# Two of eight products of an LSTM's second half, moved behind the first half's last group on TensorE

## The reference, cut to what matters

```
xW = jnp.einsum('ntd,dg->ntg', x, Wx) + b
def step(carry, xw_t):
    prev_h, prev_c = carry
    A = xw_t + prev_h @ Wh                    # Wh is 512 x 2048: gates i, f, o, g
    i, f, o = sigmoid(A[:, 0:H]), sigmoid(A[:, H:2*H]), sigmoid(A[:, 2*H:3*H])
    g = jnp.tanh(A[:, 3*H:4*H])
    next_c = f * prev_c + i * g
    next_h = o * jnp.tanh(next_c)
    return ((next_h, next_c), next_h)
```

## Time and profile before

| | |
|---|---|
| median of 3 runs | 3955.26 us |
| lowest, highest | 3949.76, 3957.27 us |
| the profiled execution | 3956.3 us |
| its span in the trace | 3954.5 us |
| TensorE's granted clock, mean | 0.994 of full speed |

### The profile page before, as it was taken

How to read it: one execution, slowest core, us unless ns; L and a number is a source line. 1 busy time by engine, 2 the same in 40 slices (tenths; PEclk the granted TensorE clock), 3 DMA queues, 4 the chain that set the end, 5 groups by cost and what they waited for, 6 DMA issues and landing times.

```text
span 3954.5 us, 255717 instructions
## 1 busy us (share of the span) xinstructions
PE 3651.2 (92%) x110802; PEld 3082.3 (78%) x110802; DVE 3272.8 (83%) x19153; ACT 1751.2 (44%) x8244; POOL 774.6 (20%) x3624
## 2 busy tenths in 40 slices
PE   6899999999999999999999999999999999999875
PEld 4688788888888888888888888888888888877764
DVE  5588888888888888888888888888888888888766
ACT  3244444444444444444444444444444444444432
POOL 0122122222222222222222222222222222212111
PEclk8999999999999999999999999999999999999999
DMA  7100000000000000000000000000000000000000
GB/s 272 48 7 7 10 10 10 7 7 10 10 10 10 7 9 7 10 10 10 10 7 7 10 10 10 10 7 9 7 10 10 10 10 7 7 7 7 6 6 8
DMA packets 19109, 63.32 MB, mean 16 GB/s; under 512 B 3958, under 2 KB 4526, under 8 KB 14914
## 3 DMA queue, kind: packets, MB, share of 16 engines
q1 hardware_dynamic: 17692, 46.67, 3.7%
q10 hardware_dynamic: 294, 0.33, 0.0%
HBM read 38.48 MB, written 8.39 MB: 12 GB/s over the span
## 4 chain that ended last, share of the span: by engine, by line
DVE 51%; PE 44%; issue 4%; ACT 1%; DMA 1%; SPq 0%; ACTq 0%; DVEq 0%; POOL 0%; POOLq 0%
PE ps_lstm L1013 34%; DVE lstm_sums L738 18%; DVE lstm_arg L743 7%; DVE lstm_ig_fc L749 6%; DVE rnn_sums L847 5%; DVE lstm_gates_2c L754 5%; DVE lstm_h_parts L778 3%; PE ps_rnn L1052 3%; DVE lstm_h_scaled L771 2%; DVE lstm_h_parts L774 2%; PE ps_lstm_in_b L1094 2%; PE ps_ssm L1094 2%; PE ps_lstm_in_b L1155 1%; PE ps_lstm_in_a L1155 1%; PE ps_x L1149 1%
## 5 line engine op out<-in xcount | busy, mean ns | idle before, releaser
L1013 PE MATMUL ps_lstm<-lstm_Wh_parts,lstm_h_parts 128*20 128x256 f16 x65472 | 1972.1, 273 | 252.2 <-DVE lstm_h_parts L778 247.3
L1013 PEld LDWEIGHTS ps_lstm<-lstm_Wh_parts,lstm_h_parts 128*20 128x20 f16 x65472 | 1543.8, 91 | 648.2 <-DVE lstm_h_parts L778 486.4
L738 DVE STREAM_TRANSPOSE lstm_sums<-ps_lstm 128x256 f32<-128x256 f32 x2048 | 912.0, 445 | 201.7 <-PE ps_lstm L1013 169.6
L486 ACT ACTIVATE lstm_gates_2c<-lstm_arg 128x32 f32<-128x32 f32 x2048 | 470.0, 230 | 1361.7 <-DVE lstm_arg L743 1361.7
L347 POOL COPY lstm_sums<-lstm_in 128x32 f32<-128x32 f32 x2048 | 423.6, 210 | 1758.6 <-DVE lstm_arg L743 1750.2
L1052 PE MATMUL ps_rnn<-rnn_Wh_parts,rnn_h_parts 128*20 128x128 f16 x32736 | 641.9, 220 | 38.4 <-DVE rnn_h_parts L893 37.0
L1052 PEld LDWEIGHTS ps_rnn<-rnn_Wh_parts,rnn_h_parts 128*20 128x20 f16 x32736 | 550.4, 92 | 77.0 <-DVE rnn_h_parts L893 57.1
L743 DVE TENSOR_REDUCE lstm_arg<-lstm_sums 128x32 f32<-128x96 f32 x2048 | 537.6, 263 | 35.2
L495 ACT ACTIVATE lstm_tanh_c<-lstm_gates_2c 128x8 f32<-128x8 f32 x2048 | 410.6, 200 | 254.7 <-DVE lstm_gates_2c L754 254.7
L509 ACT ACTIVATE rnn_h<-rnn_arg 128x16 f32<-128x16 f32 x1024 | 221.1, 216 | 529.0 <-DVE rnn_arg L852 529.0
L491 ACT ACTIVATE lstm_o_scaled<-lstm_gates_2c 128x8 f32<-128x8 f32 x2048 | 428.1, 209 | 32.5
(11 more groups left out here) (181 smaller groups left out, 2703.1 us busy)
## 6 DMA issues: line engine op xcount, KB each, us to landing
layer_plus_2I<-in_L_cond_w SPq DMA_DIRECT2D x16, 1024.0 KB, 6.4
out<-out_rows SPq DMA_DIRECT2D x128, 64.0 KB, 1.9
x_rows<-in_x SPq DMA_DIRECT2D x31, 256.0 KB
lstm_Wx<-in_L_cond_Wh SPq DMA_DIRECT2D x1, 4096.0 KB, 17.6
lstm_Wx<-in_L_cond_Wx SPq DMA_DIRECT2D x1, 4096.0 KB, 13.6
layer_plus_2I<-in_L_cond_Wh SPq DMA_DIRECT2D x1, 1024.0 KB, 8.5
rnn_Wx<-in_L_cond_Wx SPq DMA_DIRECT2D x1, 1024.0 KB, 11.0
lstm_in<-in_L_cond_w SPq DMA_DIRECT2D x1, 1024.0 KB, 9.9
```

Source lines behind the costliest of these rows:

```text
L486: A.activation(gate[h][:, 0:G, :].rearrange("p g q -> p (g q)"), arg[h][:, :, :].rearrange("p g n -> p (g n)"), ACT.Tanh, scale=gate_scale ...
L738: return mark(V.transpose(tr[h][s % 2][:, :, 0:QC], psL[h][:, 0:HW].rearrange("p (g c) -> p g c", c=QC)))
L1013: ins = mm(psL[h][QC * j:QC * j + LO + NB, 0:HW], hls[:, k, :], whl[:, k, h, e, j, :], start=(k == 0 and e == 0), stop=(k == KB - 1 and e ...
```

## The change

`products` gets the bounds `first` and `end` in place of `parts`, so that a part of its eight matmuls can be issued. Half 1's `products(1, 0)` is issued in two pieces: its matmuls 0 to 5 (e=0 with all four j, e=1 with j=0 and 1) stay in front of the wait for `lstm_h_ready1`, its matmuls 6 and 7 (e=1 with j=2 and 3) stand behind the last product of half 0. The operands, the counts of instructions and the increments and waits of semaphores are the same.

```
+EARLY = 6
-                        def products(h, k, parts=(0, 1)):
-                            for e in parts:
-                                for j in range(NQ):
-                                    ins = mm(psL[h][QC * j:QC * j + LO + NB, 0:HW], hls[:, k, :], whl[:, k, h, e, j, :],
-                                             start=(k == 0 and e == 0), stop=(k == KB - 1 and e == 1), tile_position=(0, QC * j))
+                        def products(h, k, first=0, end=2 * NQ):
+                            for q in range(first, end):
+                                e, j = q // NQ, q % NQ
+                                ins = mm(psL[h][QC * j:QC * j + LO + NB, 0:HW], hls[:, k, :], whl[:, k, h, e, j, :],
+                                         start=(k == 0 and e == 0), stop=(k == KB - 1 and e == 1), tile_position=(0, QC * j))
                             return ins
                         products(0, 0)
                         products(0, 1)
-                        products(1, 0)
+                        products(1, 0, end=EARLY)
                         if s == 0 and p["lstm"]:
                             pe.wait_ge(S_last["lstm_h_ready1"], CT)
                         elif s > 0:
                             pe.wait_ge(S["lstm_h_ready1"], s)
                         products(0, 2)
                         products(0, 3).then_inc(S["lstm_mm0"], 1)
+                        products(1, 0, first=EARLY)
                         products(1, 1)
                         products(1, 2)
                         products(1, 3).then_inc(S["lstm_mm1"], 1)
```

## The result

The changed kernel takes 3990.74 us (4 runs, 3985.13 to 3994.65), the kernel before 3956.27 us in the same comparison (4 runs). The ratio is 1.0086, with a 95% interval of 1.0073 to 1.0098. It is slower, as forecast, but by 34 us and not by 85. The profiled execution took 3994.65 us with a span of 3992.8, which is 38.3 us more than the span before.

A forecast was written before the change was run, and what follows sets the result against it. The prediction took the LSTM step-to-step loop as the bound: 27 steps at 0.08 us plus 5 at 0.109 us, 2.7 us a chunk, 86.6 us over 32 chunks, giving 4040 us; range 3975 to 4068, its own 4030 to 4067.

The forecast's parts named there:

- What bounds the kernel: Step-to-step LSTM loop, no single engine; 3.62 us a step, TensorE working in 16 rounds of 0.109 us.
- Half 0 unmoved: At lstm_mm0: half 0's last product still begins in round 10, so its end moves by 0.
- It begins in that order: TensorE: matmuls begin in program order, so half 0's last product stays in round 10 behind lanes 0 and 1.
- is not filled: Lanes 2 and 3's free slot in round 6 stays empty; half 1 ends a round, 0.109 us, later.
- rival 2: Lanes 2 and 3 run ahead, filling 0.06 of the 0.109 us hole; half 1 0.05 us later, 3980 us; chance 7%.
- In the steps where TensorE is late: First steps of a chunk, five taken per chunk: TensorE is the limit and pays the full 0.109 us each.
- Slack in front of the second transpose: Between half 1's matmuls and its VectorE transpose: 0.01 us of slack, so the transpose comes 0.10 us later.
- 0.02 us absorbed at L749: VectorE's products of half 0's gates wait for ScalarE, absorbing 0.02 us; L749 and half 1's reduction 0.08 us later.
- The sum: Whole kernel: 27 x 0.08 + 5 x 0.109 = 2.7 us a chunk, 86.6 us over 32 chunks.
- The floor of 25 ns: Skill's matmul start-to-start floor on TensorE; would make two fewer worth 0.05 us to half 0; the prediction rejected it.

The follow-up runs named there:

- one round more: Kernel before, with four matmuls of half 1 (block 1, high part), one per lane, issued twice behind half 0's last group: 4060.38 us, ratio 1.0258.
- the run with the other pair moved: Changed kernel, but the two matmuls moved behind half 0's last group are those of lanes 0 and 1, not 2 and 3: 3998.24 us, ratio 1.0100.
- two matmuls fewer: Changed kernel with the two moved matmuls not issued at all: 3951.04 us, ratio 0.9994 to the kernel before.
- moving both ends: Kernel before, half 1's first-group low-part products cut at column 128, second halves behind half 0, and four later half 1 matmuls left out: 3917.1 us, ratio 0.9893.
- a hole of a whole round: Changed kernel, with half 1's first-group matmuls reordered in front of the wait, leaving lanes 2 and 3 a round-4 hole: 3954.39 us, ratio 1.0004.

## Why the prediction was wrong

- **What bounds the kernel**: right. The loop over steps, rounds of 0.109 us per lane, and half 1's end as the point where the change would tell.
- **Half 0 unmoved**: right in its result (the transpose at 1.33 against 1.32 us), half right in its reason. Lanes 2 and 3 reach their last matmul of half 0 earlier; the release waits for lanes 0 and 1.
- **"It begins in that order", the free slot "is not filled"**: wrong, and this is the step that failed. The hole is filled once half 1's h is there. Half 1's delay is 0.05 us and not 0.109. This was rival 2, given 7%, and its sizes for TensorE hold: 64 matmuls in 1.98 us where it said 1.97. I took program order for the starts from a trace in which every lane always had the same count, and where order and independence can't be told apart. I had written so, and should have given rival 2 more.
- **In the steps where TensorE is late**: I charged 0.109 us, 17 us in all. The traces show 1.6 us in all, since half 1's h is there and the hole is filled whole. (The period of 3.93 us was read off the chain, whose piece begins at 1956.53; by TensorE's timeline the head is at 1956.46 and the period 3.86. It enters no term.)
- **Slack in front of the second transpose**: taken as 0.01 us, and the transpose does begin only 0.10 us later for a round of 0.109 (one round more). But it gives 0.01 back by lasting longer once it waits, so nothing of the slack is left. The changed kernel's transpose begins 0.031 us later and lasts 0.009 longer, 0.04 together, where the modelled ends of the matmuls say 0.05; that last 0.01 lies in the release and is open.
- **0.02 us absorbed at L749**: wrong. The reduction of half 1 waits for the transpose's end, not for L749. That this would have been visible is the lesson of the earlier trace rows: the transpose at 2002.80 with 0.44 us ends at 2003.24, and the reduction begins at 2003.27, as 2002.13 + 0.45 leads to 2002.62. L749 itself gave way by less than 0.01 us: it begins 0.38 us after the transpose before the change, and 0.37 behind a transpose that waited. With 0.04 us in this place rival 2's own sum would have been (27 x 0.04 + 5 x 0.05) x 32 = 43 us, 3998 us, and it gave 3980: its second term, for the late steps, was wrong too.
- **The sum**: 85 us against 34. With the terms put right, the second transpose's end 0.04 us later, no absorption, and nothing for the late steps: 27 x 32 x 0.04 = 35 us. That the time went the way forecast is no support for the mechanism: rival 2 went the same way.
- **The rule of the Trainium skill** (TensorE: Matmul & The Clock Gate, "What overlaps and what doesn't"), that matmuls start and end in program order: the trace after disagrees on the starts of matmuls in different column groups (0.61 before 0.66 us) and agrees on the release (the run with the other pair moved). The floor of 25 ns from start to start (same page, "Wait — 56ns, not 53.3ns?") does not hold across lanes: the four matmuls of a round begin within some 0.01 us (0.29 us for four against 0.28 for one), and two matmuls fewer gave 0.9994.

## What to carry to other kernels

Count the work per column group and not per matmul, and ask of each group when its next weights arrive: a hole costs only what no ready weights can fill. When two ends that feed one engine stand within a few hundredths of a microsecond of each other, expect nothing from moving work between them: here every version that put work later lost, and only moving both ends shortened the usual step. A wait that follows in the order of an engine is no cushion if the next instruction behind it waits for the delayed result itself.

## What the runs showed of the hardware

- A matmul can begin ahead of earlier ones of other column groups: 0.05 us ahead in the changed kernel, and with ready weights a hole of a whole round is filled (3954.39 us, where program order would give 4067).
- The release by a semaphore still waits for the matmuls that stand earlier in the program: lane 3's increment was held for lanes 0 and 1 (transpose at 2.02 us after the head and not 1.99, though its own matmul began as early as before).
- A VectorE transpose of 128x256 that had to wait for TensorE lasts 0.45 us, one that follows its predecessor directly 0.44 us (the table above). A reduction that waits for its result begins some 0.03 us after its end in all eleven traces.
